# Layer 0 of a four-layer graph network: scores and maximum found while edges are spread, and a plain compare in the edge stage

## What is computed

```python
h = x @ W_w + W_b
row, col = src, dst
e = h[row] @ a_src + h[col] @ a_dst + a_b
e = leaky_relu(e, 0.01)
attention = softmax(e, axis=0)          # over all edges
out = segment_sum(attention * h[col], row, num_segments=6250)
```

## Time and profile before

| | us |
|---|---|
| median of 3 runs | 11844.06 (11843.0 to 11853.68) |
| span of the profiled execution, first to last instruction | 10283.7 |
| spread stage, first scatter to the end of the last | 544.9 to 2763.7 |
| layer 0's edge stage | 2770.3 to 3780.6 |
| layer 1 to layer 3 | from 3784 on |

### The profile page before, as it was taken

How to read it: one execution, slowest core, us unless ns; L and a number is a source line. 1 busy time by engine, 2 the same in 40 slices (tenths; PEclk the granted TensorE clock), 3 DMA queues, 4 the chain that set the end, 5 groups by cost and what they waited for, 6 DMA issues and landing times. The chain is left out here.

```text
span 10283.7 us, 161996 instructions
## 1 busy us (share of the span) xinstructions
PE 6978.8 (68%) x46439; PEld 5971.3 (58%) x46440; DVE 6132.2 (60%) x14585; ACT 2692.4 (26%) x4442; POOL 5216.0 (51%) x5267
## 2 busy tenths in 40 slices
PE   3543334443377757778877763999984888888885
PEld 2243333333377655666666652666654888888885
DVE  8832222222277776666666654777776666666665
ACT  5022222222255562222222212444441000000000
POOL 0067777777500007777777752000003777777773
PEclk7766666666688878999999986999996666666665
DMA  4055454545544435555555571000002333333335
GB/s 167 13 154 156 157 157 156 157 155 158 154 122 121 120 97 158 148 149 152 152 154 152 155 124 54 0 0 0 0 1 64 104 103 106 106 104 103 104 108 82
DMA packets 1150548, 1137.43 MB, mean 111 GB/s; under 512 B 239363, under 2 KB 959825, under 8 KB 1150117
## 3 DMA queue, kind: packets, MB, share of 16 engines
q1 hardware_dynamic: 948422, 666.82, 23.0%
q0 software_dynamic: 195904, 465.66, 16.7%
q10 hardware_dynamic: 6048, 2.84, 0.1%
HBM read 731.30 MB, written 403.51 MB: 110 GB/s over the span
## 5 line engine op out<-in xcount | busy, mean ns | idle before, releaser
L1051 POOL DMA_INDIRECT buf<-node_rows,buf x1728 | 1745.0, 1010 | 527.5 <-issue 526.3
L1563 POOL DMA_INDIRECT buf<-node_rows_ln,buf x1728 | 1715.5, 993 | 563.4 <-issue 498.0
L717 POOL DMA_INDIRECT edge_rows_by_src<-buf x1728 | 1692.6, 980 | 550.8 <-issue 526.1
L1081 PE MATMUL psum<-buf 128*128 128x128 f32 x1728 | 368.9, 369 | 1306.2 <-DVE buf L1044 1306.2
L1081 PEld LDWEIGHTS psum<-buf 128*128 128x128 f32 x1728 | 300.0, 197 | 1326.6 <-issue 1326.6
L2066 PE MATMUL psum<-parts,buf 128*128 x4896 | 917.2, 329 | 99.5 <-DVE buf L2102 44.8
L809 DVE COPY buf<-buf 128x32 int32<-128x32 int32 x108 | 19.9, 185 | 1469.5 <-DMA buf<-records_by_dst 1469.3
L2044 ACT CAST buf<-psum 128x1024 bf16<-128x1024 f32 x612 | 619.2, 1012 | 693.0 <-PE psum L2055 693.0
L2082 DVE TENSOR_TENSOR buf<-buf,ends_of 128x2048 bf16<-128x2048 bf16 x616 | 727.0, 1222 | 111.5 <-issue 111.5
L2447 PE MATMUL psum<-buf 128*128 128x5 f32 x3456 | 747.9, 354 | 49.3 <-ACT buf L2424 49.3
L2447 PEld LDWEIGHTS psum<-buf 128*128 128x128 f32 x3456 | 738.3, 329 | 63.3 <-ACT buf L2424 63.3
(11 more groups left out here) (431 smaller groups left out, 14202.6 us busy)
## 6 DMA issues: line engine op xcount, KB each, us to landing
buf<-edge_rows_by_src SPq DMA_DIRECT2D x114, 1056.0 KB
buf<-edge_rows_by_src SPq DMA_DIRECT2D x110, 1024.0 KB
buf<-in_edge_attr SPq DMA_DIRECT2D x864, 128.0 KB
running_weighted_sums<-buf SPq DMA_DIRECT2D x108, 544.0 KB, 3.5
buf<-loc_rows_by_src SPq DMA_DIRECT2D x110, 512.0 KB, 5.1
buf<-loc_rows_by_dst SPq DMA_DIRECT2D x110, 512.0 KB, 4.6
running_sums<-buf SPq DMA_DIRECT2D x108, 512.0 KB
edge_rows_by_src<-buf SPq DMA_DIRECT2D x139, 260.0 KB, 2.8
```

Of the source, the lines that this page charges most:

```text
L717: nc.gpsimd.indirect_dma_start(rows, bass.IndirectOffsetOnAxis(ap=at[:, h, t:t + 1], axis=0), st[:, h, t, :], None).then_inc(scattered[h], 16)
L1051: nc.gpsimd.indirect_dma_start(rows[:, t, 0:used], None, table, bass.IndirectOffsetOnAxis(ap=stage[:, t:t + 1], axis=0)).then_inc(sem, 16)
L1081: last = nc.tensor.transpose(psT[:, sg % 2, t * P:(t + 1) * P], oh[:, 4 * sg + t, :], c["ident"][:])
L1563: nc.gpsimd.indirect_dma_start(xn[:, j, t, :], None, table1, bass.IndirectOffsetOnAxis(ap=stage[:, j // 4, at:at + 1], axis=0)).then_inc(g ...
```

## The change

The scores of layer 0 and their maximum move from `l0_edges` to `spread_phase`. There VectorE makes two bf16 compares of 2048 elements per half, for dst and for src, in place of 16 fp32 ones; TensorE turns both kinds in bf16, multiplies dst selections with `tab` as before, and src selections with the three parts of all 49 blocks (`find`, 48 products of 49 columns). VectorE compares each edge's block with the block numbers (`of_blk`), picks the one of 49 values and sums (`picked`, `score`), adds the dst part and the bias, applies the slope, and writes the score into the row that is stored, in the place of the dst part. Places of half n+1 come before scores of half n. A maximum per partition runs along (`most`), and is made one number, `negm`, at the end. GpSimd waits for `placed`, which now comes after the score, and no longer for `evacuated`.

In `l0_edges` a round is one half of 16 tiles, in four buffers. ScalarE takes the exponential of the stored score with the final maximum, and multiplies the 129 numbers of each row with it in place, 16 activations. VectorE makes one compare of 2048 elements, bf16 in and fp32 out, and the eight additions as before. The turns, the src products, the running maximum and the rescaling are gone. The bodies of the loops have four rounds; VectorE's first and last four stand outside its loop, of 25 passes.

```diff
...
+        negm = a_src[:, 0, :]
...
+    SCORE = D + D + 1
...
-                        pool.wait_ge(evacuated, 4 * n + 6)
...
+                def keep_dst(n, g):
+                    act.wait_ge(dst_turned, 2 * n + (g + 5))
+                    act.wait_ge(expanded, 8 * n + (4 * g + 4))
+                    nc.scalar.copy(dstT[:, g, :], psT[:, 0, :]).then_inc(dst_kept, 1)
+                def keep_src(n, g):
+                    act.wait_ge(src_turned, 2 * n + (g + 5))
+                    act.wait_ge(scored, 2 * n + (g + 1))
+                    nc.scalar.copy(srcT[:, g, :], psT[:, 1, :]).then_inc(src_kept, 1)
+                def evacuate(n, h, x):
+                    act.wait_ge(expanded, 8 * n + (x + 9))
+                    nc.scalar.copy(st[:, h, 2 * x:2 * x + 2, D:D + WT], psX[:, x % 2, 0:2 * WT].rearrange("p (t k) -> p t k", t=2)).then_inc(evacuated, 1)
...
+                        keep_dst(n, 0)
+                        keep_src(n, 0)
+                        keep_dst(n, 1)
+                        for x in range(4):
+                            evacuate(n, h, x)
+                        keep_src(n, 1)
+                        for x in range(4, 8):
+                            evacuate(n, h, x)
...
+                        def find(g):
+                            pe.wait_ge(src_kept, 2 * n + (g + 2))
+                            for t in range(G):
+                                for k in range(3):
+                                    last = nc.tensor.matmul(psS[:, g, t * NB:(t + 1) * NB], srcT[:, g, t * P:(t + 1) * P], parts[:, k, :], start=(k == 0), stop=(k == 2))
+                            last.then_inc(scored, 1)
...
+                        pe.wait_ge(dst_kept, 2 * n + 1)
+                        turn(0, 0, dst_turned)
+                        pe.wait_ge(src_kept, 2 * n + 1)
+                        turn(1, 0, src_turned)
+                        pe.wait_ge(dst_kept, 2 * n + 2)
+                        turn(0, 1, dst_turned)
+                        for x in range(4):
+                            expand(x)
+                        pe.wait_ge(src_kept, 2 * n + 2)
+                        turn(1, 1, src_turned)
+                        pe.wait_ge(chosen, n + 1)
+                        find(0)
+                        pe.wait_ge(dst_kept, 2 * n + 3)
+                        for x in range(4, 8):
+                            expand(x)
+                        find(1)
...
+                def find_places(n, h, i):
...
+                    dve.wait_ge(rec_got[h], 128 * i + 128)
+                    nc.vector.tensor_copy(st[:, h, :, ROW - 2:ROW].bitcast(I32), rec[:, h, :, 2:4])
+                    lp.link(nc.vector.tensor_copy(locs[:, b, 1, :], field(2).bitcast(F32)))
+                    lp.link(nc.vector.tensor_copy(place[:], field(3)))
...
+                    lp.link(nc.vector.tensor_scalar(locs[:, b, 0, :], place[:], -1.0, None, ALU.add))
+                    dve.wait_ge(dst_turned, 2 * n + 2)
+                    dve.wait_ge(src_turned, 2 * n + 2)
+                    for w in range(2):
+                        last = nc.vector.tensor_tensor(sel[:, b, w], bc(iota[:].unsqueeze(1), [P, PAIRS, P, 2]),
+                                                       bc(locs[:, b, w, :].rearrange("p (a t) -> p a t", t=2).unsqueeze(2), [P, PAIRS, P, 2]), ALU.is_equal)
+                    last.then_inc(hot, 1)
+                    lp.link(nc.vector.tensor_copy(node[:], field(1)))
+                    lp.link(nc.vector.tensor_tensor(key[:], node[:], field(2).bitcast(F32), ALU.subtract))
+                    lp.link(nc.vector.tensor_tensor(of_blk[:, b], blk_no[:], bc(key[:].unsqueeze(1), [P, NB, HALF]), ALU.is_equal))
+                    lp.link(nc.vector.tensor_scalar(lost[:, b], valid[:], -1.0, -NEG, ALU.add, ALU.mult))
+                    lp.link(nc.vector.scalar_tensor_tensor(node[:], node[:], float(-DUMMY), valid[:], ALU.add, ALU.mult))
...
+                    lp.link(nc.vector.tensor_tensor(at[:, h, :], node[:], spare, ALU.add))
...
+                def find_scores(n, h, after):
...
+                    dve.wait_ge(scored, 2 * n + 4)
+                    lp.link(nc.vector.tensor_tensor(picked[:].rearrange("p (g t) k -> p g t k", g=2), psS[:, :, 0:G * NB].rearrange("p g (t k) -> p g t k", t=G),
+                                                    of_blk[:, b].rearrange("p k (g t) -> p g t k", g=2), ALU.mult))
+                    dve.sem_inc(chosen, 1)
+                    lp.link(nc.vector.tensor_reduce(score[:], picked[:], AX.X, ALU.add))
+                    dve.wait_ge(evacuated, 8 * n + 10)
+                    lp.link(nc.vector.scalar_tensor_tensor(score[:], score[:], ab[:], of_dst, ALU.add, ALU.add))
+                    lp.link(nc.vector.scalar_tensor_tensor(of_dst, score[:], 0.01, score[:], ALU.mult, ALU.max))
+                    dve.sem_inc(placed, 1)
+                    lp.link(nc.vector.tensor_tensor(cand[:], of_dst, lost[:, b], ALU.add))
+                    lp.link(nc.vector.tensor_tensor(most[:], most[:], cand[:], ALU.max))
...
+                def step(i, h):
+                    n = R * i + h
+                    if not isinstance(i, int) or n + 1 < NH:
+                        find_places(n + 1, (h + 1) % R, i if h + 1 < R else i + 1)
+                    if not isinstance(i, int) or n >= 0:
+                        if isinstance(i, int) and n == NH - 1:
+                            dve.sem_inc(kept, 1)
+                        find_scores(n, h, 1 if isinstance(i, int) and n == NH - 1 else 2)
...
+                nc.vector.tensor_reduce(top[:], most[:], AX.X, ALU.max).then_inc(maxed, 1)
...
+                nc.vector.tensor_scalar(negm, psM[:, P:P + 1], -1.0, None, ALU.mult)
...
+                with act.Fori(0, NI) as i:
+                    for s in range(R):
+                        n = R * i + s
+                        act.wait_ge(got[s], 16 * i + 16)
+                        nc.scalar.activation(p[:, s % 2, :], rows[:, s, :, D + 1:D + 2].rearrange("p t o -> p (t o)"), ACT.Exp, bias=negm).then_inc(weights, 1)
...
+                        for t in range(HALF):
+                            last = nc.scalar.activation(rows[:, s, t, 0:D + 1], rows[:, s, t, 0:D + 1], ACT.Copy, scale=p[:, s % 2, t:t + 1])
+                        last.then_inc(weighed, 1)
...
+                def weigh(n, s, i):
+                    dve.wait_ge(got[s], 16 * i + 16)
+                    nc.vector.tensor_copy(locs[:, s % 2, :].unsqueeze(2), rows[:, s, :, W - 2:W - 1]).then_inc(picked, 1)
+                    if not isinstance(n, int) or n >= 2:
+                        dve.wait_ge(summed, n - 1)
+                    dve.wait_ge(picked, n + 1)
+                    nc.vector.tensor_tensor(oh[:, s % 2], bc(iota[:].unsqueeze(1), [P, PAIRS, P, 2]),
+                                            bc(locs[:, s % 2, :].rearrange("p (a t) -> p a t", t=2).unsqueeze(2), [P, PAIRS, P, 2]), ALU.is_equal).then_inc(hot, 1)
...
+                def add(n, s, i):
+                    blocks = pair_blocks(nc, ENG.DVE, blk, i, s, 0, R)
+                    dve.wait_ge(partly, n + 1)
...
+                        if q == 3:
+                            dve.wait_ge(summed, n + 1)
+                        dve.wait_ge(added, PAIRS * n + (PAIRS + q + 1))
...
+                with dve.Fori(1, NI - 1) as i:
+                    for s in range(R):
+                        weigh(R * i + (s + 1), (s + 1) % R, i + (s + 1) // R)
+                        add(R * i + s, s, i)
...
```

More of the change, by code:

```diff
@@ L655, in spread_phase @@
         dump, place, valid, node = sb([P, R * HALF]), sb([P, HALF]), sb([P, HALF]), sb([P, HALF])
+        numbers, lost, score, cand, most = sb([P, NB]), sb([P, 2, HALF]), sb([P, HALF]), sb([P, HALF]), sb([P, HALF])
+        ab, top, top1 = sb([P, 1]), sb([P, 1]), sb([1, 1])
         idx2, loc2 = c["idx"], c["loc"]
-        psT = es.enter_context(nc.psum_tensor(fresh("psum"), [P, 2, 512], F32))
-        psX = es.enter_context(nc.psum_tensor(fresh("psum"), [P, 2, 2, 512], F32))
-        loaded, consts, dve_chain, based, hot, turned, ohT_ready, expanded, evacuated, placed, gathering, kept = (sem() for _ in range(12))
@@ L663, in spread_phase, with over_bodies @@
         rec_got, edge_got, scattered = ([sem() for _ in range(R)] for _ in range(3))
-        DV = 13
+        PLACE, SCORED = 17, 6
+        NI = NH // R
+        def over_bodies(eng, step, first):
+            for h in range(R + first, R):
+                step(-1, h)
+            with eng.Fori(0, NI - 1) as i:
+                for h in range(R):
+                    step(i, h)
+            for h in range(R):
+                step(NI - 1, h)
         with nc.Block() as block:
@@ L755, in _ @@
                         blocks = pair_blocks(nc, ENG.PE, blk_b, i, h, 0, R)
-                        def expand(g):
-                            pe.wait_ge(ohT_ready, 4 * n + (g + 3))
-                            pe.wait_ge(evacuated, 4 * n + (g + 1))
```

(24 more changed lines are left out.)

383 lines of the change are left out of this document (115 added, 268 removed).

## The result

The kernel before took 11846.0 us (20 runs), the changed one 11879.8 (20 runs): ratio 1.0025, 95% interval 1.0015 to 1.0035. It is slower by some 34 us, clear of no change but small; 316 faster had been predicted. The profiled execution of after took 11876.34 us with a span of 11874.5, so nothing but 1.8 us lies outside the trace. The 1560 us that the prediction put there were something else, which the first experiment shows.

What follows compares the result with a forecast made beforehand. GpSimd was taken to bound the spread stage and VectorE layer 0's edge stage. Terms -377 (edge stage), +8 (start) and +53 (GpSimd slowed) sum to -316: 11844 to 11528 us, range 11420 to 11670.

Steps and rivals of the forecast that it cites:

- The base: Whole kernel: the 1560 us between span 10283.7 and median 11844 lie outside the trace and stay fixed.
- The spread stage's bound: Spread stage: GpSimd keeps binding at 20.5 us per 16 tiles; VectorE 8.8, ScalarE 7.2, TensorE 16 to 17 fit under it.
- rival (e): Spread stage: the scores' chain takes over 20.5 us per round and sets the pace; at 24 all gain is lost; chance 0.02.
- Waits: Spread stage: GpSimd's permission comes about 34 us after an earlier scatter, needed after 62, so it costs only at the start.
- Layer 0's edge stage: Layer 0's edge stage: VectorE binds at 5.7 us per 16 tiles, 633 us against 1010.2, 377 us gained.
- Rival (a): Layer 0's edge stage: dearer rounds, by activations at 0.39 (11646 us) or register loads not hidden (11615); chance 0.17.
- (d): Faster: edge compare takes 1.23 us, ScalarE binds at 5.5, GpSimd is slowed by the lower end; 11463 us; chance 0.07.
- GpSimd beside VectorE: Spread stage: new VectorE work slows GpSimd's scatters by 0.073 us per us, 53 us lost, range 10 to 150.
- rival (b): Spread stage: GpSimd held longer, each of two compares holding a scatter for 0.77 us; 97 us more, 11625; chance 0.13.
- Rival (c): Spread stage: every two-input VectorE operation holds GpSimd for its whole length, 408 us lost, slower at 11883; chance 0.03.
- The start: Spread stage: first scatter moves from 544.99 to 553 us, as places of two rounds and scores come first; 8 us lost.
- Untouched stages: Stages the change doesn't touch: expected not to move; if one did, the whole forecast would be wrong.

Runs made afterwards that it cites:

- the first experiment: The kernels before and after, both unchanged, profiled once more on one chip: 12058.2 us (span 12056.3) and 12110.0 us (span 12108.1).
- before_again: The kernel before, unchanged, profiled once more on a slow chip: 12058.2 us, span 12056.3.
- after_again: The changed kernel, unchanged, profiled once more on the same slow chip as before_again: 12110.0 us, span 12108.1.
- not_waited: Changed kernel with the score put in a buffer that isn't stored, so GpSimd needn't wait for it: ratio to before 0.9983 slow, 0.9703 and 0.9715 quick.
- after_third: The changed kernel, unchanged, on a quick chip beside wide_pause: 9996.1 us against 10284.3 for before, ratio 0.9714.
- wide: Changed kernel with destination products copied four tiles at a time instead of two: ratio to before 0.9719 on a quick chip, 0.9921 on a slow one.
- wide_pause: wide, plus GpSimd waiting mid-group until its first eight scatters have landed, on a quick chip: 10220.1 us against 10284.3 for before, ratio 0.9932.

## Why the prediction was wrong

**The base.** "the 1560 us between lie outside the trace. I hold them fixed". This step failed. By its span the profile was of the quick kind and the runs were of the slow one, less than 2 us lies outside the traces taken since, and 547 of the 1773 us sit in the very stage that got new work. The span was 13% short of the three times beside it. The sentence "The whole would be wrong if the time outside the span moved too" named the danger, but I gave it no chance of its own.

**The spread stage's bound.** "All under 20.5", and rival (e) with 0.02: the scores' chain of a round takes over 20.5 us and sets the pace. On quick chips the step was right: "issue" alone between scatters, ratio 0.971 to 0.972. On slow chips the chain set the pace already before the change, at 25.6 us per group, and with the scores it is 29.0 to 29.4. The gaps between groups of scatters are 20% of the stage in before_again and hold 203 of ScalarE's 457 busy us and 119 of TensorE's 976; in after_again they are 29% and hold 428 of 692 and 525 of 1103 (from the fifth group on). So much of the added work isn't done beside the scatters. Rival (e) is what happened: its point was 3.5 us per group over the pace of before (24 against 20.5), and 3.8 were measured, +410 us against -387 for the edge part on one slow chip. What holds the work up beside the scatters stays open.

**Waits.** "GpSimd needs it after three rounds", so the later permission costs only at the start. Right on quick chips. On slow ones not_waited puts it at some 77 us of 410.

**Layer 0's edge stage.** Predicted 377 us, with 5.7 per 16 tiles bound by VectorE. Measured 5.65, and 377.6 (quick) and 386.8 (slow) for the whole part up to layer 1's first gather. The unknown prices went as taken: activations at 0.30 as said, no hold by register loads, 0.3 us more in a round at the loop's return, the compare 2.29 (2.20 was taken, which was the distance of two starts; L1290 itself took 2.28). Rival (a) falls, and (d), which needed a compare of 1.23. What I had missed is a table load of 1.28 us on ScalarE once per pass of the loop's body, so every fourth round; VectorE's bound hides it. The granted clock was expected to be lower here and rose, from 0.83 to 0.89 on quick chips; as said, it decides nothing while VectorE binds.

**GpSimd beside VectorE.** Predicted 53, range 10 to 150. Measured 91 on quick chips. That GpSimd is held beside VectorE was right, and the term too small: 0.073 us per us of VectorE averages over many operations, but it is the two compares that hold one scatter by 1 us, 0.84 us per 16. This is about half of rival (b), which had each compare hold one. Rival (c), a hold for the whole length of every two-input operation, falls: during the 108 picked products (L917, 1.6 us, where 0.97 had been estimated) of after_third 207 scatters started, and none took over 1.3 us. The rule of the skill weighed there (the Trainium skill, "SBUF — State Buffer", Who interferes with whom) fits the compares, with one scatter of 1.95 us beside 2.36 us of compares. For the picked product, which reads one operand from PSUM, the same section says that an instruction with at most one SBUF input doesn't contend with GpSimd outside the 2-port perf modes; the trace agrees. The comparison of keys (L901, 0.57 us, both inputs in SBUF) decides nothing: in each of the 106 rounds in which one met a scatter, the scatter had begun first.

**The start.** Predicted +8, measured +5.5 and +6.5.

**Untouched stages.** Held at nothing; -16 on quick chips, +22 between the two single executions on a slow one, both about what a repeat gives.

The sum for a quick chip was -316 against -287 measured. For a slow chip the same parts give -386.8 + 6.5 + 410.4 + 21.7 = +51.8 (spans 12056.3 and 12108.1), and the result's medians +34. A slip in the text changes nothing: rival (c) decides from 3.6 us per round and not 3.4, once the 16 us of before are taken off as in its own sum.

**What is better than both.** wide: on a quick chip 0.9719 of before, like the changed kernel; on a slow one 0.9921, where the changed one has 1.0025 in the result.

## What to carry to other kernels

Compare the span of a profile with the timed runs before any sum is made. Here later profiles came within 2 us of their time; where a span is off by more than repeated runs are, the profile may be of something else than what is timed, and the stages in which it could differ are the first rival. An engine that is "free" beside a stream of indirect transfers is free only if its work was seen to go on beside them on the chip in question; count the handovers and instructions that it gets, and keep them few. And a price averaged over a stage hides which operation pays it: look for the longest scatters and what stands beside them.

## What the runs showed of the hardware

- The same program takes 10277 to 10293 us on three chips and 11841 to 12058 on three others. 1769 of 1773 us lie in the stages with one indirect transfer per tile. What makes a chip the one or the other, and whether it stays so, isn't shown by any run here.
- On slow chips GpSimd itself issues as fast as on quick ones (median scatter 0.97 us on both); what is late is the work of the others: small products 2.1 us apart instead of 0.03, VectorE idle for 1.1 to 2.1 us of "issue" between small operations, a semaphore's update 18 to 20 us behind its product, 2.5 us after the last scatter's end. Whether instructions, their data or the updates are held wasn't told apart.
- A pause of GpSimd until its transfers have landed shortens such a stage on a slow chip (by some 170 of 3127 us, between two sets of runs) and lengthens it on a quick one (by 234 of 2306 us, wide_pause against wide).
- From the last scatter to layer 1's first gather the granted clock is 0.82 in before_again and 0.90 in after (slow chips), 0.83 and 0.89 on quick ones, while TensorE's busy time in it is 741.87 us of 1110.8 and 459.13 of 725.1.
- Beside two compares with both inputs in SBUF (2.36 us together) one scatter takes 1.95 us instead of 0.97; none of 207 scatters that started during a product with one input in PSUM was held.
